# A score tile's maximum, minimum and squares one tile per step, with TensorE's side work between scores and weighted sum

## The chip, the cores and the metric

One core of one Trainium2 chip runs the kernel. The metric is the device time of one launch in microseconds (us).

## The reference

Sixteen sequences of 1024 token ids go through a small tower, in fp32:

```python
h = tok(x)          # embedding, 128x128, six gated convolutions (kernel 3), 128x128
h = h + attn(layernorm(h))
h = h + ffn(layernorm(h))

# attn: 8 heads of 16, two score maps
attn1 = softmax(q1 @ k1.T * scale); attn2 = softmax(q2 @ k2.T * scale)
# per window of 4 rows and head: mean, std, max, min over the 1024 keys of each map
gate_in = concat([window_stats(attn1, 4), window_stats(attn2, 4)])
alpha = sigmoid(mlp(gate_in))
out = ((alpha * attn1 + (1 - alpha) * attn2) @ v) @ Wo
```

The ffn part is a layer norm, a 128x128 product with a residual, one expert's two products with a gelu between, and a last product with a gelu.

## The kernel before

The five engines each run a program written out by hand; semaphores tie them together. The work on one sequence is a body of 128 steps: 16 units (8 heads, two score maps) of 8 row tiles of 128 queries. The loop runs over 16 sequences. Beside the attention of sequence i each step also carries side tasks: the tail of the sequence before (window statistics, gate, ffn: `POST`) and the front of the next one (embedding, convolutions `conva` and `convg`, q and k: `PRE`). `plan()` puts them into steps and isn't changed. It gives 95 of the 128 steps a side task on TensorE; steps 50 to 79 all have one.

A step n of the main work has these parts:
- `scores`: TensorE makes a 128x1024 score tile in one of two halves of `ps_s` (buffer n % 2), as two matmuls.
- `row_max`, `row_min` on VectorE: the tile's maximum and minimum. `squares` on ScalarE: exp of the tile minus its maximum, with its sum (`junk`, `sumsq`), an activation and a read of the accumulator.
- `scores_t`: TensorE makes the transposed scores of the tile 12 steps earlier in `ps_t`, again two matmuls; there is one `ps_t`. `exp_t` on ScalarE takes them to `exps`.
- `weighted`: TensorE multiplies `exps` of two steps earlier with v and adds into `ps_o`.
- side tasks of `STEP[n]`: on TensorE they write `ps_w`, a single bank. `wait_bank` makes each of them wait until the task before it has been read: by ScalarE (`va`, `ug`, `hpre`, `stage` and others) or, for eight kinds, by VectorE.

Before, two steps form a pair. VectorE takes both maxima, then both minima; ScalarE's squares stand between maximum and minimum of a tile. TensorE's order in a pair is scores, scores_t, scores, side task, scores_t, weighted twice, side task. A tile of `ps_s` is free for new scores when its minimum is through. `scores_t` and `exp_t` count in halves of 512 columns. SyncE's queue brings the units' q and k (12 transfers each) and the maxima as three rows (`mrow`); GpSimd has the elementwise part of the side tasks.

Of the kernel before, what the change touches and what calls it, by code (L numbers as in the profile page):

```python
# [24 lines left out]
P = 128  # L25
L = 1024
T = L // P
# [133 lines left out]
def tower_kernel(nc, ids, table, consts, w_e2h, b_e2h, conv_w, conv_b, w_h2e, b_h2e, wq1, wk1, wq2, wk2, wv, wo,  # L161
# [4 lines left out]
    with ExitStack() as ctx:  # L166
# [149 lines left out]
        def _(sp):  # L316
# [41 lines left out]
            with sp.Fori(0, NB // E) as group, sp.Fori(0, E) as e:  # L358
                i = group * E + e
                sp.wait_ge(s_emb, i * (16 * T) + 16 * T)  # L360
                settle()
                load_ids(i + 1)
                load_expert("body", i, e)
                for j in range(U):

                    if j:
                        sp.wait_ge(s_st, i * (2 * STEPS) + 2 * (T * (j - 3) + T - 1 + LAG_T) + 2)
                    else:
                        sp.wait_ge(s_exp, i * (2 * STEPS) + 2)
                    settle()  # L370
                    store_mrow("body", i, j)
                    if j + 1 in (U // 2, U):
                        wait_side(sp, "body", i, "pool", QK[(j + 1) % U // H][-1])
                        settle()
                    load_unit((j + 1) % U)
                    if ("gelu2",) in sum((STEP[n] for n in range(j * T, j * T + T)), []):
                        store_out("body", i)
# [7 lines left out]
        def _(pe):  # L385
# [3 lines left out]
            def scores(i, n):  # L389

                u, t = n // T, n % T
                if t == 0:
                    pe.wait_ge(s_ring[u % RING], i * (4 * 12 * 16) + 12 * 16 * (u // RING + 1))
                pe.wait_ge(s_min, i * STEPS + n + 1)
                for c in range(2):
# [4 lines left out]
            def scores_t(i, n):  # L400

                m = (n - LAG_T) % STEPS
                u, t = m // T, m % T
                if t == 0:
                    pe.wait_ge(s_mrow, i * (U * 64) + 64 * (n // T + 2))
                for c in range(2):
                    pe.wait_ge(s_exp, i * (2 * STEPS) + 2 * n + c + 1)
                    mm(ps_t[:, c, :], kst[:, u % RING, P * t:P * t + P], qst[:, u % RING, 512 * c:512 * c + 512])\
                        .then_inc(s_st, 1)

            def weighted(i, n, count=True):
# [3 lines left out]
                if count:  # L415
                    pe.wait_ge(s_exp, i * (2 * STEPS) + max(2 * n, 1))
                    if t == 0:
# [131 lines left out]
            with pe.Fori(0, NB // E) as group, pe.Fori(0, E) as e:  # L549
                i = group * E + e  # L550
                for n in range(0, STEPS, 2):
                    scores(i, n)
                    scores_t(i, n)
                    scores(i, n + 1)
                    for tk in STEP[n]:
                        task("body", i, tk)
                    scores_t(i, n + 1)
                    weighted(i, n)
                    weighted(i, n + 1)
                    for tk in STEP[n + 1]:  # L560
                        task("body", i, tk)
            for n in range(LAG_V):
# [8 lines left out]
        def _(act):  # L571
            def squares(i, n):

                r, t = n // T % RING, n % T
                if t == 0:

                    wait_side(act, "body", i, "pool", ("unit", n // T - 2) if n // T > 1 else None)
                act.wait_ge(s_max, i * STEPS + n + 1)
                act.wait_ge(s_sq, i * STEPS + n + 1)
# [3 lines left out]
            def exp_t(i, n):  # L583
                act.wait_ge(s_pv, i * STEPS + n + 1)
                for c in range(2):
                    act.wait_ge(s_st, i * (2 * STEPS) + 2 * n + c + 1)
                    nc.scalar.activation(exps[:, n % RING, 512 * c:512 * c + 512], ps_t[:, c, :], ACT.Exp,  # L587
                                         scale=0.5).then_inc(s_exp, 1)

# [89 lines left out]
            act.sem_inc(s_sq, 2)  # L679
            act.sem_inc(s_exp, 2)  # L680
            act.sem_inc(s_mrow, 64)
            for tk in PRE:
                task("pre", 0, tk)
            with act.Fori(0, NB // E) as group, act.Fori(0, E) as e:
                i = group * E + e
                for n in range(0, STEPS, 2):
                    exp_t(i, n)
                    squares(i, n)
                    for tk in STEP[n]:
                        task("body", i, tk)  # L690
                    squares(i, n + 1)
                    exp_t(i, n + 1)
                    for tk in STEP[n + 1]:
                        task("body", i, tk)
            for n in range(LAG_T):
# [6 lines left out]
        def _(dve):  # L702
# [17 lines left out]
            def row_min(i, n):  # L720
                r, t = n // T % RING, n % T
                dve.wait_ge(s_sq, i * STEPS + n + 3)
                nc.vector.tensor_reduce(rowmin[:, r, t:t + 1], ps_s[:, n % 2, :], axis=AX, op=ALU.min)\  # L723
# [106 lines left out]
            last.then_inc(s_init, 1)  # L830
            dve.sem_inc(s_min, 2)
            dve.sem_inc(s_out, 16)
# [5 lines left out]
            with dve.Fori(0, NB // E) as group, dve.Fori(0, E) as e:  # L838
                i = group * E + e
                for n in range(0, STEPS, 2):  # L840

                    row_max(i, n)
                    row_max(i, n + 1)
                    for tk in STEP[n]:
                        task("body", i, tk)
                    row_min(i, n)
                    row_min(i, n + 1)
                    for tk in STEP[n + 1]:
                        task("body", i, tk)
# [232 lines left out]
```

## Time and profile before

| | us |
|---|---|
| runs | 6308.97, 6310.05, 6312.23; median 6310.05 |
| span of the profiled execution | 6310.3 |
| TensorE, VectorE, ScalarE, GpSimd busy | 5419.2, 5358.7, 5292.3, 2425.1 |
| mean granted TensorE clock | 0.927 of full speed |

The profiled execution is one of its own; its span stands within 0.01% of the median of the runs, so sums against its times may be read against the runs as well. Times of the trace count from the start of the span. A granted clock of 1.00 is 2.4 GHz, 0.50 is 1.2 GHz.

### The profile page before, as it was taken

What the parts mean: (1) busy time and instruction counts of PE and PEld (TensorE: products, weight loads), DVE (VectorE), ACT (ScalarE), POOL (GpSimd) and SP (SyncE); (2) the same over time, 40 slices, a digit from 0 to 9 for tenths busy, and PEclk for the clock granted to TensorE, in tenths of its full rate; (3) what the DMA queues carried; (4) which work ended last, traced back from release to release, by engine and by line L of the source; (5) the groups of instructions that cost most, each with busy time, mean ns of one, the idle gap of its engine ahead of it and who ended that gap; (6) DMA issues with size and microseconds to landing.
All of it is one profiled execution on the core that took longest, in us unless ns stands there. A gap on an engine that the chain in (4) does not pass through costs nothing.

```text
span 6310.3 us, 127411 instructions
## 1 busy us (share of the span) xinstructions
PE 5419.2 (86%) x34070; PEld 2706.4 (43%) x34070; DVE 5358.7 (85%) x6524; ACT 5292.3 (84%) x9997; POOL 2425.1 (38%) x4629
## 2 busy tenths in 40 slices
PE   6988889889888888889889888888889888898886
PEld 4443434444343443434444343443434444343443
DVE  2888888898988888888898888888889888888883
ACT  2888888889888888888889888888888888888884
POOL 6424343342433424343342433424344242433422
PEclk8999989999998999989999898999999999898997
DMA  1001010010101001010010101001010010101000
GB/s 37 19 20 26 19 28 19 20 27 22 26 19 28 19 20 26 18 28 19 20 27 22 26 19 28 18 21 26 18 28 19 20 26 22 25 19 27 19 22 12
DMA packets 165102, 142.52 MB, mean 23 GB/s; under 512 B 89197, under 2 KB 108269, under 8 KB 164141
## 3 DMA queue, kind: packets, MB, share of 16 engines
q1 hardware_dynamic: 159100, 124.09, 8.5%
q0 software_dynamic: 4352, 8.92, 0.7%
q8 instruction: 325, 5.32, 0.4%
q14 instruction: 509, 4.16, 0.2%
q10 hardware_dynamic: 816, 0.02, 0.0%
HBM read 21.26 MB, written 8.91 MB: 5 GB/s over the span
## 4 chain that ended last, share of the span: by engine, by line
PE 40%; issue 22%; DVE 18%; ACT 14%; POOL 3%; ACTq 1%; SPq 1%; DMA 0%; DVEq 0%; POOLq 0%
PE ps_w L387 18%; PE ps_s L387 8%; DVE negmax L717 7%; PE ps_t L387 7%; ACT junk L580 7%; PE ps_o L387 6%; DVE rowmin L723 4%; ACT exps L587 4%; DVE o_t L732 1%; DVE bn L742 1%; ACT hpre L636 1%; DVE mean_all L736 1%; DVE recip L735 1%; PE ps_w L435 1%; SPq L329 1%
## 5 line engine op out<-in xcount | busy, mean ns | idle before, releaser
L723 DVE TENSOR_REDUCE rowmin<-ps_s 128x1 f32<-128x1024 f32 x2048 | 2479.1, 1221 | 559.8 <-ACT junk L580 468.0
L580 ACT ACTIVATE junk<-ps_s,negmax 128x1024 bf16<-128x1024 f32 x2048 | 2300.9, 1124 | 473.2 <-DVE negmax L717 438.2
L717 DVE TENSOR_REDUCE negmax<-ps_s 128x1 f32<-128x1024 f32 x2048 | 2412.9, 1215 | 156.0 <-PE ps_s L387 128.1
L587 ACT ACTIVATE exps<-ps_t 128x512 f32<-128x512 f32 x4120 | 2265.7, 615 | 230.7 <-PE ps_t L387 211.8
L387 PE MATMUL ps_s<-kst,qst 96*128 96x512 bf16 x4096 | 1329.3, 408 | 486.7 <-DVE rowmin L723 421.0
L387 PE MATMUL ps_t<-qst,kst 99*128 99x512 bf16 x4120 | 1442.9, 408 | 220.6 <-ACT exps L587 165.7
L387 PE MATMUL ps_w<-xc,cw 128*128 128x256 f32 x4704 | 1253.5, 404 | 22.0 <-ACT ug L656 12.4
L387 PE MATMUL ps_o<-exps,v_cur 128*32 128x256 f32 x16512 | 1161.6, 401 | 20.4 <-POOL v_cur L1012 20.3
L387 PEld LDWEIGHTS ps_w<-xc,cw 128*128 128x128 f32 x4704 | 902.8, 199 | 354.2 <-issue 117.2
L387 PEld LDWEIGHTS ps_t<-qst,kst 99*128 99x128 bf16 x4120 | 414.8, 101 | 1120.9 <-ACT exps L587 877.0
L871 POOL TENSOR_SCALAR ctmp<-ug 128x256 f32<-128x256 f32 x408 | 165.9, 407 | 1569.0 <-ACT ug L656 1561.0
L387 PEld LDWEIGHTS ps_s<-kst,qst 96*128 96x128 bf16 x4096 | 322.5, 101 | 1022.9 <-DVE rowmin L723 849.6
L387 PEld LDWEIGHTS ps_o<-exps,v_cur 128*32 128x32 f32 x16512 | 442.6, 112 | 634.1 <-issue 443.3
L580 ACT ACTIVATION_READ_ACCUMULATOR junk<-ps_s,negmax 128x1 f32 x2048 | 429.4, 210 | 0.0
L987 POOL TENSOR_TENSOR ctmp<-ctmp,va 128x256 f32<-128x256 f32 x408 | 296.7, 727 | 33.9
L988 POOL TENSOR_TENSOR ctmp<-ctmp,xc 128x256 f32<-128x256 f32 x408 | 278.8, 683 | 32.0
L884 POOL TENSOR_TENSOR dif_all<-rowmin,negmax 128x8 f32<-128x8 f32 x258 | 52.7, 204 | 578.9 <-DVE o_all L737 565.9
L591 ACT ACTIVATE va<-ps_w,cb 128x256 f32<-128x256 f32 x392 | 190.5, 486 | 61.8 <-PE ps_w L387 50.4
L656 ACT ACTIVATE ug<-ps_w,cb_half 128x256 f32<-128x256 f32 x392 | 190.7, 486 | 53.2 <-PE ps_w L387 51.3
L871 POOL TENSOR_SCALAR part<-stage 128x512 bf16<-128x512 f32 x132 | 82.1, 622 | 368.4 <-ACT stage L591 359.8
L871 POOL TENSOR_SCALAR xc<-ctmp 128x256 f32<-128x256 f32 x408 | 167.6, 411 | 65.3 <-POOL ctmp L988 65.3
L905 POOL DMA_INDIRECT att<-in_table,idx x136 | 131.5, 967 | 135.2 <-DMA idx<-in_ids 95.7
(179 smaller groups left out, 4147.6 us busy)
## 6 DMA issues: line engine op xcount, KB each, us to landing
qst<-part SPq DMA_DIRECT2D x1542, 32.0 KB, 2.0
kst<-part SPq DMA_DIRECT2D x1542, 32.0 KB, 2.0
qst<-mrow SPq DMA_DIRECT2D x1028, 1.5 KB
out_dram<-z SPq DMA_DIRECT2D x17, 512.0 KB, 3.2
fc1s<-in_fc_w SPq DMA_DIRECT2D x17, 256.0 KB
fc2s<-in_fc_w SPq DMA_DIRECT2D x17, 256.0 KB
cw<-in_conv_w SPq DMA_DIRECT2D x1, 2304.0 KB
att<-in_table,idx POOLq DMA_INDIRECT x136
```

Source lines behind the costliest of these rows:

```text
L329: sp.dma_start(dst[HD * g:HD * g + HD, r, :], part[HD * h:HD * h + HD, a, w, c, :])\
L387: return nc.tensor.matmul(dst, lhs, rhs, start=start, stop=stop, **kw)
L580: nc.scalar.activation(junk[:, n % 2, :], ps_s[:, n % 2, :], ACT.Exp, bias=negmax[:, r, t:t + 1], accum_out=sumsq[:, r, t:t + 1]).then_inc ...
L587: nc.scalar.activation(exps[:, n % RING, 512 * c:512 * c + 512], ps_t[:, c, :], ACT.Exp, scale=0.5).then_inc(s_exp, 1)
L591: return nc.scalar.activation(dst, src, ACT.Identity, **kw)
L656: last = nc.scalar.activation(ug[:, c % 2, :], bank[:, CH:2 * CH], ACT.Tanh, scale=0.5, bias=cb_half[:, 2 * l + 1:2 * l + 2])
L717: nc.vector.tensor_reduce(negmax[:, r, t:t + 1], ps_s[:, n % 2, :], axis=AX, op=ALU.max, negate=True)\
L723: nc.vector.tensor_reduce(rowmin[:, r, t:t + 1], ps_s[:, n % 2, :], axis=AX, op=ALU.min)\
L871: return nc.gpsimd.tensor_scalar(*args)
L905: nc.gpsimd.indirect_dma_start(out=emb[:, t, :], out_offset=None, in_=table[:, :], in_offset=bass.IndirectOffsetOnAxis(ap=idx[:, t:t + 1], ...
L987: chain(i, tt(ctmp[:, 1, :], ctmp[:, 0, :], va[:, c % 2, :], ALU.mult))
L988: chain(i, tt(ctmp[:, 2, :], ctmp[:, 1, :], x_in, ALU.add))
```

## The change

A tile now goes maximum, minimum, squares, and a step is one tile. VectorE's `row_min` no longer waits for anything of its own (it follows `row_max` on the same tile); `squares` waits for the minimum; `scores` waits for the squares of two steps earlier, which now is the last reader of the tile. `scores_t` and `exp_t` are counted once for a step; `exp_t` is one activation of 1024 columns instead of two of 512. TensorE's order in each step is scores, side tasks, weighted, scores_t; ScalarE's is exp_t, side tasks, squares. The initial counts and SyncE's waits follow.

```diff
--- before.py
+++ after.py
@@ -364,9 +364,9 @@
                 for j in range(U):
 
                     if j:
-                        sp.wait_ge(s_st, i * (2 * STEPS) + 2 * (T * (j - 3) + T - 1 + LAG_T) + 2)
+                        sp.wait_ge(s_st, i * STEPS + T * (j - 3) + T + LAG_T)
                     else:
-                        sp.wait_ge(s_exp, i * (2 * STEPS) + 2)
+                        sp.wait_ge(s_exp, i * STEPS + 1)
                     settle()
                     store_mrow("body", i, j)
                     if j + 1 in (U // 2, U):
@@ -391,7 +391,7 @@
                 u, t = n // T, n % T
                 if t == 0:
                     pe.wait_ge(s_ring[u % RING], i * (4 * 12 * 16) + 12 * 16 * (u // RING + 1))
-                pe.wait_ge(s_min, i * STEPS + n + 1)
+                pe.wait_ge(s_sq, i * STEPS + n + 1)
                 for c in range(2):
                     last = mm(ps_s[:, n % 2, 512 * c:512 * c + 512], qst[0:KSC, u % RING, P * t:P * t + P],
                               kst[0:KSC, u % RING, 512 * c:512 * c + 512])
@@ -403,17 +403,18 @@
                 u, t = m // T, m % T
                 if t == 0:
                     pe.wait_ge(s_mrow, i * (U * 64) + 64 * (n // T + 2))
+                pe.wait_ge(s_exp, i * STEPS + n + 1)
                 for c in range(2):
-                    pe.wait_ge(s_exp, i * (2 * STEPS) + 2 * n + c + 1)
-                    mm(ps_t[:, c, :], kst[:, u % RING, P * t:P * t + P], qst[:, u % RING, 512 * c:512 * c + 512])\
-                        .then_inc(s_st, 1)
+                    last = mm(ps_t[:, c, :], kst[:, u % RING, P * t:P * t + P],
+                              qst[:, u % RING, 512 * c:512 * c + 512])
+                last.then_inc(s_st, 1)
 
             def weighted(i, n, count=True):
 
                 m = (n - LAG_V) % STEPS
                 h, t = m // T % H, m % T
                 if count:
-                    pe.wait_ge(s_exp, i * (2 * STEPS) + max(2 * n, 1))
+                    pe.wait_ge(s_exp, i * STEPS + max(n, 1))
                     if t == 0:
                         pe.wait_ge(s_ot, i * U + n // T + 1)
                     if m == 0:
@@ -548,17 +549,12 @@
             wait_side(pe, "body", 0, "dve")
             with pe.Fori(0, NB // E) as group, pe.Fori(0, E) as e:
                 i = group * E + e
-                for n in range(0, STEPS, 2):
+                for n in range(STEPS):
                     scores(i, n)
-                    scores_t(i, n)
-                    scores(i, n + 1)
                     for tk in STEP[n]:
                         task("body", i, tk)
-                    scores_t(i, n + 1)
                     weighted(i, n)
-                    weighted(i, n + 1)
-                    for tk in STEP[n + 1]:
-                        task("body", i, tk)
+                    scores_t(i, n)
             for n in range(LAG_V):
                 if n < LAG_T:
                     scores_t(NB, n)
@@ -575,17 +571,16 @@
                 if t == 0:
 
                     wait_side(act, "body", i, "pool", ("unit", n // T - 2) if n // T > 1 else None)
-                act.wait_ge(s_max, i * STEPS + n + 1)
+                act.wait_ge(s_min, i * STEPS + n + 1)
                 act.wait_ge(s_sq, i * STEPS + n + 1)
                 nc.scalar.activation(junk[:, n % 2, :], ps_s[:, n % 2, :], ACT.Exp, bias=negmax[:, r, t:t + 1],
                                      accum_out=sumsq[:, r, t:t + 1]).then_inc(s_sq, 1)
 
             def exp_t(i, n):
                 act.wait_ge(s_pv, i * STEPS + n + 1)
-                for c in range(2):
-                    act.wait_ge(s_st, i * (2 * STEPS) + 2 * n + c + 1)
-                    nc.scalar.activation(exps[:, n % RING, 512 * c:512 * c + 512], ps_t[:, c, :], ACT.Exp,
-                                         scale=0.5).then_inc(s_exp, 1)
+                act.wait_ge(s_st, i * STEPS + n + 1)
+                nc.scalar.activation(exps[:, n % RING, :], ps_t[:, :, :].rearrange("p c q -> p (c q)"), ACT.Exp,
+                                     scale=0.5).then_inc(s_exp, 1)
 
             def ident_act(dst, src, **kw):
                 return nc.scalar.activation(dst, src, ACT.Identity, **kw)
@@ -677,21 +672,17 @@
             nc.scalar.activation(cb_half[:, :], cb[:, :], ACT.Copy, scale=0.5).then_inc(s_init, 1)
             act.wait_ge(s_init, 4)
             act.sem_inc(s_sq, 2)
-            act.sem_inc(s_exp, 2)
+            act.sem_inc(s_exp, 1)
             act.sem_inc(s_mrow, 64)
             for tk in PRE:
                 task("pre", 0, tk)
             with act.Fori(0, NB // E) as group, act.Fori(0, E) as e:
                 i = group * E + e
-                for n in range(0, STEPS, 2):
+                for n in range(STEPS):
                     exp_t(i, n)
-                    squares(i, n)
                     for tk in STEP[n]:
                         task("body", i, tk)
-                    squares(i, n + 1)
-                    exp_t(i, n + 1)
-                    for tk in STEP[n + 1]:
-                        task("body", i, tk)
+                    squares(i, n)
             for n in range(LAG_T):
                 exp_t(NB, n)
             for tk in TAIL:
@@ -719,7 +710,6 @@
 
             def row_min(i, n):
                 r, t = n // T % RING, n % T
-                dve.wait_ge(s_sq, i * STEPS + n + 3)
                 nc.vector.tensor_reduce(rowmin[:, r, t:t + 1], ps_s[:, n % 2, :], axis=AX, op=ALU.min)\
                     .then_inc(s_min, 1)
 
@@ -828,7 +818,6 @@
 
             last = nc.vector.memset(kst[KSC:KST, :, :], 1.0)
             last.then_inc(s_init, 1)
-            dve.sem_inc(s_min, 2)
             dve.sem_inc(s_out, 16)
             dve.wait_ge(s_load, 16 * N_LOADS)
             dve.wait_ge(s_init, 4)
@@ -837,15 +826,10 @@
             pos.update(loop=True, base=pos["n"], n=0, per=U + 3)
             with dve.Fori(0, NB // E) as group, dve.Fori(0, E) as e:
                 i = group * E + e
-                for n in range(0, STEPS, 2):
-
+                for n in range(STEPS):
                     row_max(i, n)
-                    row_max(i, n + 1)
+                    row_min(i, n)
                     for tk in STEP[n]:
-                        task("body", i, tk)
-                    row_min(i, n)
-                    row_min(i, n + 1)
-                    for tk in STEP[n + 1]:
                         task("body", i, tk)
             assert pos["n"] == pos["per"], pos
             pos.update(n=0)
```

What the order on TensorE looks like, before, where a convolution half (`ps_w<-xc,cw`) and a product of fc1 (`ps_w<-xa,fc1s`) stand in neighbouring steps, about the middle of the body (REGISTER_ALU and ISA rows work out and make waits):

```order
L394 REGISTER_ALU
L387 MATMUL ps_s<-kst,qst 128x512 x2
L273 REGISTER_ALU
L387 MATMUL ps_w<-xc,cw 128x256 x3
L407 REGISTER_ALU
L387 MATMUL ps_t<-qst,kst 128x512
L407 REGISTER_ALU
L387 MATMUL ps_t<-qst,kst 128x512
L387 MATMUL ps_o<-exps,v_cur 32x256 x8
L273 REGISTER_ALU
L387 MATMUL ps_w<-xa,fc1s 128x256 x2
```

And after the change, at such a place:

```order
L387 MATMUL ps_s<-kst,qst 128x512 x2
L273 REGISTER_ALU x2
L387 MATMUL ps_w<-xc,cw 128x256 x3
L419 REGISTER_ALU
L387 MATMUL ps_o<-exps,v_cur 32x256 x4
L387 MATMUL ps_t<-qst,kst 128x512 x2
L394 REGISTER_ALU
L387 MATMUL ps_s<-kst,qst 128x512 x2
L273 REGISTER_ALU
L387 MATMUL ps_w<-xa,fc1s 128x256 x2
L387 MATMUL ps_o<-exps,v_cur 32x256 x4
L387 MATMUL ps_t<-qst,kst 128x512 x2
```

The matmuls of weighted (`ps_o`) and of scores_t (`ps_t`) stood between the two side tasks for both steps of the pair; now scores_t of step n and scores of step n + 1 stand ahead of the side task of step n + 1, and weighted and scores_t of that step behind it.

ScalarE, before, the same two tasks' activations (`ug` for the convolution half, `hpre` for fc1):

```order
L580 ACTIVATE junk,sumsq<-ps_s,negmax 128x1024
L273 REGISTER_ALU
L656 ACTIVATE ug<-ps_w,cb_half 128x256
L578 REGISTER_ALU
L580 ACTIVATE junk,sumsq<-ps_s,negmax 128x1024
L586 REGISTER_ALU
L587 ACTIVATE exps<-ps_t 128x512
L586 REGISTER_ALU
L587 ACTIVATE exps<-ps_t 128x512
L273 REGISTER_ALU
L591 ACTIVATE hpre<-ps_w,fc1bs 128x256 x2
```

And after (line numbers are those of the changed file):

```order
L582 ACTIVATE exps<-ps_t 128x1024
L273 REGISTER_ALU
L651 ACTIVATE ug<-ps_w,cb_half 128x256
L576 ACTIVATE junk,sumsq<-ps_s,negmax 128x1024
L580 REGISTER_ALU
L582 ACTIVATE exps<-ps_t 128x1024
L273 REGISTER_ALU
L586 ACTIVATE hpre<-ps_w,fc1bs 128x256 x2
L576 ACTIVATE junk,sumsq<-ps_s,negmax 128x1024
```

The activation that reads the side bank stood behind the squares in the first step of a pair and behind exp_t in the second; now it stands behind exp_t in every step.

## Rows read from the trace of the kernel before

**Rows 1.** The page: span, engines, granted clock by slice

```profile
span 6310.3 us, 127411 instructions
...
PE 5419.2 (86%) x34070; PEld 2706.4 (43%) x34070; DVE 5358.7 (85%) x6524; ACT 5292.3 (84%) x9997; POOL 2425.1 (38%) x4629
...
PEclk8999989999998999989999898999999999898997
```

**Rows 2.** Busy time in four stretches; each row begins with the stretch and its length

```profile
core 0: us, PE busy (x) PEld busy (x) DVE busy (x) ACT busy (x) POOL busy (x), PEclk, DMA share, GB/s
0.00:138.30 138.30, 82.60 (x367) 65.86 (x368) 17.00 (x43) 29.48 (x61) 86.35 (x135) 0.86 0.12 31
3168.80:3548.00 379.20, 329.77 (x2092) 162.35 (x2090) 332.86 (x402) 327.91 (x619) 144.54 (x279) 0.94 0.10 23
3312.30:3396.30 84.00, 81.35 (x522) 44.88 (x520) 74.77 (x79) 77.75 (x157) 27.18 (x62) 0.98 0.09 20
6202.70:6310.30 107.60, 56.32 (x330) 37.31 (x330) 12.89 (x51) 37.15 (x66) 25.94 (x31) 0.71 0.03 10
```

**Rows 3.** The list of waits: who waited for whom, µs, times, longest

```profile
PEld ps_s L387 <- DVE rowmin L723: 849.6, 1306, 4.3
...
ACT junk L580 <- DVE negmax L717: 438.2, 484, 2.6
...
PEld ps_w L387 <- ACT va L591: 70.3, 104, 0.9
```

**Rows 4.** Timeline with side work in every step: start, length, engine, line

```profile
3384.56 1.01 ACT L591 ACTIVATE hpre<-ps_w,fc1bs 128x256 f32<-128x256 f32 x2
...
3385.04 2.35 DVE L717 TENSOR_REDUCE negmax<-ps_s 128x1 f32<-128x1024 f32 x2
...
3385.22 0.60 PE L387 MATMUL ps_s<-kst,qst 96*128 96x512 bf16 x2
...
3385.28 1.26 ACT L587 ACTIVATE exps<-ps_t 128x512 f32<-128x512 f32 x2
3385.63 1.16 PEld L387 LDWEIGHTS ps_w<-xc,cw 128*128 128x128 f32 x6 [0.30 <-ACT hpre L591]
3385.66 1.53 PE L387 MATMUL ps_w<-xc,cw 128*128 128x256 f32 x6
...
3386.29 1.26 ACT L580 ACTIVATE junk<-ps_s,negmax 128x1024 bf16<-128x1024 f32 x1
...
3387.03 0.60 PE L387 MATMUL ps_t<-qst,kst 99*128 99x512 bf16 x2
...
3387.31 0.34 ACT L580 ACTIVATION_READ_ACCUMULATOR junk<-ps_s,negmax 128x1 f32 x1
3387.40 0.61 ACT L656 ACTIVATE ug<-ps_w,cb_half 128x256 f32<-128x256 f32 x1
...
3387.55 1.07 PE L387 MATMUL ps_o<-exps,v_cur 128*32 128x256 f32 x16
...
3388.55 1.13 PE L387 MATMUL ps_w<-xa,fc1s 128*128 128x256 f32 x4
...
3388.84 1.24 ACT L587 ACTIVATE exps<-ps_t 128x512 f32<-128x512 f32 x2
...
3389.52 0.60 PE L387 MATMUL ps_s<-kst,qst 96*128 96x512 bf16 x2
...
3389.80 1.01 ACT L591 ACTIVATE hpre<-ps_w,fc1bs 128x256 f32<-128x256 f32 x2
```

**Rows 5.** The costliest groups on the page: busy µs, mean ns

```profile
L656 ACT ACTIVATE ug<-ps_w,cb_half 128x256 f32<-128x256 f32 x392 | 190.7, 486 | 53.2 <-PE ps_w L387 51.3
```

**Rows 6.** Timeline at gelu1 and just behind it

```profile
3398.99 1.28 ACT L636 ACT_TABLE_LOAD   x1
...
3400.29 3.89 ACT L636 ACTIVATE hpre<-hpre 128x1024 f32<-128x1024 f32 x4
...
3408.98 2.77 PE L387 MATMUL ps_w<-xc,cw 128*128 128x256 f32 x6
```

## The prediction

> **What bounds the kernel now.** I read the page's shares first: VectorE, ScalarE and TensorE are busy 85, 84 and 86% of a span of 6310.3 us, so no engine is the bound by itself; what counts is how they wait for each other [rows 1]. The stretches come next: a prologue of 138.3 us, a tail of 107.6 us, and between them 16 equal blocks of 379.2 us, 128 steps each, 2.96 us a step [rows 2]. One stretch inside a block is of special use: steps 50 to 79, in each of which TensorE has a side task, take 84.0 us, 2.80 us a step [rows 2].
>
> The list of waits says where the order bites: scores wait for the row minimum (849.6 us), the squares for the row maximum (438.2 us) [rows 3]. The timeline shows one pair of steps: both maxima (2.35 us), squares, squares, minimum, minimum. The reader is to see in it that TensorE hardly ever waits for its side bank ps_w. The convolution at 3385.66 started 0.09 us after the end of the hpre activation that empties the bank (3384.56 + 1.01), and the weight load had waited 0.30 us for it [rows 4]. Over the whole run such a wait for the va activations costs 70.3 us in 104 times [rows 3]: it is nearly free, because the pairwise order leaves a whole step between the read of the bank and the next task.
>
> **The change part by part.**
>
> *Score order.* VectorE now runs maximum and minimum of one tile, 2.35 us for two such reductions [rows 4], and the squares come last. A tile's circle is scores, maximum, minimum, squares: 0.64 + 2.35 + 0.04 + 1.36 + 0.05 us. 0.64 is 0.60 for two matmuls [rows 4] and a hand-over of 0.04; 1.36 is from the squares' start to the end of the accumulator's read (3386.29 to 3387.65) [rows 4]. That is 4.4 us over two tiles, so the score engine pair could run at 2.35 us a step. The waits of [rows 3] on rowmin go away as such.
>
> *Merged exponential.* Two activations of 512 columns become one of 1024. The two take 0.96 us until the next activation starts (3388.84 to 3389.80) [rows 4]; four activations of 128x1024 take 3.89 us with a last one of about a full length, so at most 0.97 us each [rows 6]. I cost the merge at nothing. The bounds: the merged one may need 0.96 or, by the squares' length, 1.26 us [rows 4]; the far end is 0.3 us a step dearer. A step on the Trainium skill, apart from the sum: ScalarE: Activation LUTs, section "What ACT_TABLE_LOAD costs", puts an activation with immediate operands at 186 ns plus 0.833 ns an element, with 93 ns of overlap. By that an estimate of two halves is 1.04 us and of one whole 0.95 us, which would give back about 0.09 us a step; the trace's 0.96 against at most 0.97 doesn't bear this out.
>
> *One instead of two counts for the halves.* scores_t now waits for the whole of the previous exponential and the exponential for both matmuls of scores_t. Before, the halves were handed over one by one. From the start of scores_t to that of the exponential it is now 0.64 us (0.60 for two matmuls and 0.04) [rows 4].
>
> *TensorE's side work.* This decides, and it is the step where I expect the loss. The new order on TensorE is scores, side task, weighted, scores_t; on ScalarE exponential, side task, squares. There is one side bank ps_w, and each task on TensorE waits until the previous task's reader is through. So where steps n and n+1 both have a task that ScalarE reads, there is a circle of ONE step: scores_t(n), exponential(n), ScalarE's side task(n), then TensorE's side task(n+1), weighted(n+1), scores_t(n+1). Queued behind the waiting side task are weighted and scores_t, and the next exponential waits for those. Its price, all from [rows 4] unless said:
> - 0.64 scores_t to exponential; 0.96 exponential to the side activation;
> - the side activation: 0.49 (ug) [rows 5], or 1.01 for the two of hpre;
> - 0.06 hand-over (0.09 at most, above);
> - TensorE's task: 1.37 for a convolution half (3385.66 to 3387.03), 0.97 for fc1 (3388.55 to 3389.52);
> - 0.50 weighted, half of the 1.00 from 3387.55 to 3388.55.
>
> Convolution behind convolution: 0.64 + 0.96 + 0.49 + 0.06 + 1.37 + 0.50 = 4.02 us. fc1 behind convolution 3.62, convolution behind fc1 4.54, mean 4.08. Of the 127 neighbouring steps in the plan, 69 are such a pair with ScalarE as the first one's reader: 20 convolution behind convolution, 15 mixed with fc1, 34 others, whose TensorE tasks are mostly transposes or single products; for those I take the 3.62 us of the cheaper form. The mean is (35 x 4.05 + 34 x 3.62) / 69 = 3.84 us, against 2.80 us a step now [rows 2]. That is 69 x 1.04 = 72 us a block.
>
> *The other 59 steps.* They cost 379.2 - 69 x 2.80 = 186 us now. After the change 38 of them alternate, one with a task and one without: the circle over two steps is squares' end, scores 0.44 (3385.22 to 3385.66), task 1.37, weighted 0.50, then 0.64 + 0.96 + 0.49 and squares 1.36, with 0.05 of hand-over 5.8 us, a bit less with the smaller tasks; call it 2.75 us a step, 105. Seven follow a task that VectorE reads (2.75, 19). Fourteen have nothing beside them and go at VectorE's 2.35 (33). To these 157 us come the long activations with their table loads (3.89 + two of 1.28 for gelu1) [rows 6], the moments on VectorE and the slow clock behind such pauses. What they cost now is what is left of the 186 us when 59 steps have 2.62 us each (5.24 for two, 3384.56 to 3389.80) [rows 4]: about 31 us, and I keep 30. Sum 187 us: no change. Prologue and tail keep their work.
>
> *Pool, queues.* The DMAs are the same. SP's waits for scores_t and the exponential name the same steps in new counts. GpSimd's msplit has three reductions instead of four between its maximum and VectorE's mrow, over 3.5 us (three of 2.35 / 2) [rows 4], and the loads go out a whole unit of 8 steps ahead; with longer steps they have more time, not less. I cost them at nothing.
>
> *Sum.* 16 x 72 = 1150 us on top of the profiled execution's 6310.3 us gives 7460 us; the median of the runs is 6310.05, so the same number stands against it.
>
> **TensorE's clock.** Behind the gelu1 pause a convolution's six matmuls took 2.77 us [rows 6] instead of 1.53 us [rows 4]. In the new circle TensorE has 0.44 + 0.44 + 1.37 + 0.50 us to issue in 4.02 us, so it idles about 1.2 us in each. If the clock falls to 1.2 GHz there, scores_t, task and weighted roughly double and a step costs about 6.3 us. TensorE: Matmul & The Clock Gate, section "HAM oscillation — how this bites in real kernels", warns of regular idle gaps on TensorE, which is D below as a rule; no row here has this pattern. Now TensorE idles 13% of a block (329.77 of 379.20 us busy) and the granted clock is 0.94; where side work is dense it idles 3% at 0.98 [rows 2]. Neither shows what 30% in short pieces does, so D below gets a small chance and no more.
>
> **The rivals.**
> - *A, forecast:* the one-step circle through ps_w. 0.81.
> - *B, the bank wait doesn't bind* and only the two-step circle over the squares does (5.8 us for two steps, 2.9 against 2.80 now): 16 x 69 x 0.1 = +110, 6420 us, perhaps 6300 with what light steps give. For it: the wait is just 70.3 us now [rows 3]. Against: ScalarE's task moved behind the exponential that TensorE's own later work feeds. 0.06.
> - *C, faster:* ps_w is free in time and VectorE alone sets the pace: its own work in the 30 dense steps is 74.8 of 84.0 us, 0.31 us a step less [rows 2]; 16 x 69 x 0.31 = -340, so 5970 us. It decides if the side task on TensorE could start before about 2.3 us of the step are gone; here it would have to be free 1.5 us earlier than the sum says. 0.05.
> - *D, the clock falls in the runs:* a third of 69 steps at 6.3 instead of 3.84 us gives 16 x 57 = 900 on top, 8370 us. 0.08.
>
> **How the numbers follow.** Predicted 7460 us. The circle's bounds: 3.62 us if all links are of the cheap form (+900, 7210), 4.4 us if the merged exponential takes 0.3 us more and hpre's 1.01 is frequent (+1770, 8080); a gain of 0.1 us in the 59 other steps is -95. I take 7100 to 7850, which leaves B, C and D outside. A measurement of this kernel tells about 0.2% from no change. Faster has C and a sliver of B: 0.06; same 0.02; slower 0.92.
>
> **What would show it.** Right: a step of about 4 us in the stretch where side work is dense (30 steps in about 117 instead of 84.0 us); matmuls or weight loads of ps_w that wait for ScalarE's va, ug, hpre for over a microsecond each, the largest sum in the list of waits; VectorE's wait for ScalarE before rowmin gone; VectorE's share down from 85 to about 72% (85 x 6310 / 7460); steps without side work at 2.4 us. Wrong: ps_w loads that start as soon as scores are issued; or a granted clock far under 0.93, which would be D.

## The result and the profile after

The changed kernel takes 7757.4 us (median of 4 runs, 7751.06 to 7773.02), the kernel before beside it on the same chip 6309.51: a ratio of 1.2297, with a 95% interval of 1.228 to 1.2315. The forecast was 7460 us, 7100 to 7850. The profiled execution has a span of 7760.3 us at a mean granted clock of 0.940 (0.927 before).

The page of the changed kernel, to be held against [rows 1]; the L rows give busy us, mean ns, and the idle time ahead with who ended it:

```profile
span 7760.3 us, 118934 instructions
...
PE 5667.7 (73%) x34070; PEld 2477.9 (32%) x34070; DVE 5320.7 (69%) x6524; ACT 5171.0 (67%) x7937; POOL 2419.8 (31%) x4629
...
PEclk8999999999999999999999999999999999999898
...
L582 ACT ACTIVATE exps<-ps_t 128x1024 f32<-128x1024 f32 x2060 | 2112.8, 1026 | 2261.4 <-PE ps_t L387 2258.2
L713 DVE TENSOR_REDUCE rowmin<-ps_s 128x1 f32<-128x1024 f32 x2048 | 2488.4, 1215 | 0.0
```

VectorE and ScalarE have the same work as before, within 2.5%, over a longer span. What the change meant for VectorE it got: rowmin waits for nothing. But the exponentials now wait 2261 us in all, for scores_t.

The stretches of the changed kernel, one block and steps 50 to 79 of it, to be held against [rows 2]:

```profile
3880.70:4349.50 468.80, 345.92 (x2090) 148.63 (x2092) 330.67 (x403) 319.00 (x489) 144.41 (x279) 0.94 0.08 18
4059.90:4183.60 123.70, 86.95 (x509) 40.59 (x512) 74.80 (x81) 76.80 (x126) 27.05 (x62) 0.97 0.06 14
```

A block went from 379.2 to 468.8 us, and 16 x 89.6 = 1434 of the 1450 us between the two profiled executions. The 30 steps with dense side work alone went from 84.0 to 123.7 us. VectorE and ScalarE have the same 75 and 77 us of work there as before.

The list of waits, changed kernel, to be held against [rows 3]:

```profile
POOL ctmp L855 <- ACT ug L651: 2525.0, 369, 15.9
ACT exps L582 <- PE ps_t L387: 2258.2, 1518, 19.9
DVE negmax L708 <- PE ps_s L387: 2085.5, 1325, 19.8
PEld ps_s L387 <- ACT junk L576: 868.4, 643, 6.1
...
PEld ps_w L387 <- ACT va L586: 473.7, 304, 1.6
...
PE ps_w L387 <- ACT ug L651: 363.9, 336, 1.3
...
PEld ps_w L387 <- ACT ug L651: 319.9, 208, 1.7
PE ps_w L387 <- ACT va L586: 318.5, 304, 1.1
```

The wait of a ps_w weight load for va rose from 70.3 to 473.7 us. The first row is GpSimd, 31% busy, waiting for its next piece of side work. The next two look like TensorE being slow. They aren't: TensorE is idle 27% of the span. These rows pass on what TensorE itself waited for. All rows in which a matmul on ps_w waits for a ScalarE activation add up to 1260 us, against 98 before; for the weight loads of ps_w it is 1362 us against 224. Only a timeline shows where such a wait begins. Here is one pair of steps of the changed kernel, to be held against [rows 4], the idle time ahead in brackets:

```profile
4122.25 0.60 PE L387 MATMUL ps_t<-qst,kst 99*128 99x512 bf16 x2
...
4122.69 0.60 PE L387 MATMUL ps_s<-kst,qst 96*128 96x512 bf16 x2
...
4122.95 1.02 ACT L582 ACTIVATE exps<-ps_t 128x1024 f32<-128x1024 f32 x1 [1.45 <-PE ps_t L387]
...
4123.88 0.84 ACT L586 ACTIVATE hpre<-ps_w,fc1bs 128x256 f32<-128x256 f32 x2
...
4124.76 1.56 PE L387 MATMUL ps_w<-xc,cw 128*128 128x256 f32 x6 [1.47 <-ACT hpre L586]
...
4126.26 0.64 PE L387 MATMUL ps_o<-exps,v_cur 128*32 128x256 f32 x8
...
4126.83 0.61 PE L387 MATMUL ps_t<-qst,kst 99*128 99x512 bf16 x2
...
4127.53 1.02 ACT L582 ACTIVATE exps<-ps_t 128x1024 f32<-128x1024 f32 x1 [1.72 <-PE ps_t L387]
...
4128.45 0.47 ACT L586 ACTIVATE va<-ps_w,cb 128x256 f32<-128x256 f32 x1
...
4128.97 1.13 PE L387 MATMUL ps_w<-xa,fc1s 128*128 128x256 f32 x4 [1.11 <-ACT va L586]
...
4130.03 0.64 PE L387 MATMUL ps_o<-exps,v_cur 128*32 128x256 f32 x8
...
4130.61 0.61 PE L387 MATMUL ps_t<-qst,kst 99*128 99x512 bf16 x2
```

Read it as a ring (the prediction's circle through ps_w): scores_t, exponential, the activation that empties the bank, the next task on the bank, weighted, scores_t. No link has slack. TensorE stands 1.47 us ahead of one task and 1.11 ahead of the other. One round took 4.58 us (4122.25 to 4126.83), the next 3.78.

### The profile page after: what moved, and what is told of

Its sections match the earlier page's. It is cut to its first block, busy times and chain, and to the rows that moved or that the text cites. A ratio compares the mean times of both kernels' runs of the same rounds, so it can differ in the third digit from the quotient of the medians.

```text
span 7760.3 us, 118934 instructions
## 1 busy us (share of the span) xinstructions
PE 5667.7 (73%) x34070; PEld 2477.9 (32%) x34070; DVE 5320.7 (69%) x6524; ACT 5171.0 (67%) x7937; POOL 2419.8 (31%) x4629
## 3 DMA queue, kind: packets, MB, share of 16 engines
q14 instruction: 462, 3.78, 0.2%
## 4 chain that ended last, share of the span: by engine, by line
PE 51%; issue 21%; ACT 15%; DVE 6%; POOL 3%; ACTq 2%; SPq 1%; DMA 1%; POOLq 0%; DVEq 0%
PE ps_w L387 23%; PE ps_o L387 12%; PE ps_t L387 11%; PE ps_s L387 4%; DVE rowmin L713 3%; ACT ug L651 2%; ACT junk L576 2%; ACT exps L582 2%; ACT va L586 2%; ACT hpre L586 1%; SPq L329 1%; PE ps_w L436 1%; DVE negmax L708 1%; ACT stage L586 1%; DVE bn L732 1%
## 5 line engine op out<-in xcount | busy, mean ns | idle before, releaser
L708 DVE TENSOR_REDUCE negmax<-ps_s 128x1 f32<-128x1024 f32 x2048 | 2502.1, 1222 | 2093.3 <-PE ps_s L387 2085.5
L582 ACT ACTIVATE exps<-ps_t 128x1024 f32<-128x1024 f32 x2060 | 2112.8, 1026 | 2261.4 <-PE ps_t L387 2258.2
L387 PE MATMUL ps_w<-xc,cw 128*128 128x256 f32 x4704 | 1310.0, 418 | 627.7 <-ACT va L586 186.1
L387 PE MATMUL ps_o<-exps,v_cur 128*32 128x256 f32 x16512 | 1401.1, 413 | 80.8 <-DVE o_t L722 60.5
L387 PE MATMUL ps_t<-qst,kst 99*128 99x512 bf16 x4120 | 1301.5, 399 | 69.5 <-ACT exps L582 67.5
L387 PEld LDWEIGHTS ps_o<-exps,v_cur 128*32 128x32 f32 x16512 | 334.3, 111 | 868.8 <-issue 674.3
L387 PEld LDWEIGHTS ps_t<-qst,kst 99*128 99x128 bf16 x4120 | 237.2, 98 | 1010.9 <-issue 747.9
L855 POOL TENSOR_SCALAR mparts<-negmax 128x8 bf16<-128x8 f32 x256 | 51.8, 202 | 664.2 <-DVE negmax L708 631.5
L387 PE MATMUL ps_w<-xa,fc1s 128*128 128x256 f32 x524 | 147.3, 404 | 144.6 <-ACT ug L651 73.9
L722 DVE STREAM_TRANSPOSE o_t<-ps_o 128x256 f32<-128x256 f32 x258 | 115.0, 446 | 112.9 <-PE ps_o L387 110.8
L586 ACT ACTIVATE va<-ps_w,cb 128x256 f32<-128x256 f32 x392 | 184.5, 471 | 10.8 <-POOL xc L855 8.3
```

The costliest lines, as they stand in the source:

```text
L387: return nc.tensor.matmul(dst, lhs, rhs, start=start, stop=stop, **kw)
L582: nc.scalar.activation(exps[:, n % RING, :], ps_t[:, :, :].rearrange("p c q -> p (c q)"), ACT.Exp, scale=0.5).then_inc(s_exp, 1)
L586: return nc.scalar.activation(dst, src, ACT.Identity, **kw)
L708: nc.vector.tensor_reduce(negmax[:, r, t:t + 1], ps_s[:, n % 2, :], axis=AX, op=ALU.max, negate=True)\
L722: nc.vector.transpose(o_t[:, :], ps_o[:, 0:QC]).then_inc(s_ot, 1)
L855: return nc.gpsimd.tensor_scalar(*args)
```

## The experiments

Each ratio is against the kernel before on the same chip; the median of the kernel before was about 6380 us in the runs of x1 to x4 and x12, and 6306 to 6309 in the others. Edits are against the changed kernel unless said. a2 is the changed kernel again, on the chip of x9 and x10; x5 to x8 ran on another chip, whose kernel before stands within 0.1% of a2's.

**a2_changed_again.** 

> The changed kernel as it is, on the same chip as the other two of this set, so that small differences can be read: ratio 1.23 of the kernel before.

Measured: 7768.83 us, ratio 1.2312 (1.2291 to 1.2332). The result repeats.

**x1_side_behind_scores_t**, the ring opened on TensorE:

```diff
                     scores(i, n)
-                    for tk in STEP[n]:
-                        task("body", i, tk)
                     weighted(i, n)
                     scores_t(i, n)
+                    for tk in STEP[n]:
+                        task("body", i, tk)
```

> The changed kernel with one edit: TensorE's side task stands behind scores_t instead of between scores and weighted. If the one-step circle through ps_w is the cause (forecast A), it opens, because ScalarE has the whole of the next step's exponential, scores and weighted to empty the bank: a step with side work falls from 4.2 us to TensorE's own 2.8 us (0.44 + 0.5 + 0.44 + 1.4), a block from 468 to about 375 us, the whole to 6150 to 6400 us. If the two-step circle over the squares is the cause (B), little changes, since squares still stand behind the side task: 7400 to 7800 us.

Measured: 6220.53 us, ratio 0.9738 (0.9709 to 0.9766). Steps 50 to 79, and a step of them:

```profile
3268.70:3348.60 79.90, 76.75 (x508) 41.23 (x512) 74.18 (x81) 77.06 (x127) 26.98 (x61) 1.00 0.10 21
```

```profile
3300.89 0.61 PE L387 MATMUL ps_t<-qst,kst 99*128 99x512 bf16 x2
...
3301.34 1.46 PE L387 MATMUL ps_w<-xc,cw 128*128 128x256 f32 x6
...
3301.60 1.02 ACT L582 ACTIVATE exps<-ps_t 128x1024 f32<-128x1024 f32 x1 [0.47 <-PE ps_t L387]
...
3302.91 0.48 ACT L586 ACTIVATE va<-ps_w,cb 128x256 f32<-128x256 f32 x1 [0.29 <-PE ps_w L387]
```

The time lies in the 6150 to 6400 us expected of an open ring. The task now runs beside the exponential instead of behind it. The 30 steps went from 123.7 to 79.9 us, with the same instructions. Over the whole run the matmuls on ps_w wait 10 us for ScalarE, not 1260.

**x2_act_side_first**, the ring opened on ScalarE instead:

```diff
-                    exp_t(i, n)
                     for tk in STEP[n]:
                         task("body", i, tk)
+                    exp_t(i, n)
                     squares(i, n)
```

> The changed kernel with one edit on the other engine: ScalarE does its side task ahead of exp_t, TensorE's order stays. If the circle through ps_w is the cause, the link scores_t to exponential to side activation leaves it, the bank is read right behind TensorE's task, and the time falls to 6200 to 6600 us, near x1. If instead TensorE's side task costs because it delays scores_t itself, the time stays above 7000 us.

Measured: 6315.99 us, ratio 0.9887 (0.9858 to 0.9916). The side activation goes ahead of the exponential, and the loss is gone too. Two edits on two engines, with no line in common, each take back all of it; what they share is the ring. TensorE's side task still stands ahead of scores_t in x2, so its place there alone isn't what costs.

**x5_dose_in_circle and x6_dose_outside.** One more activation of 128x256, in the 48 steps with a convolution: in x5 ahead of the side activation, inside the ring, in x6 behind it, ahead of the squares. (The line that declares the buffer `extra` is left out here.)

```diff
                     exp_t(i, n)
+                    if any(tk[0] in ("conva", "convg") for tk in STEP[n]):      # x5
+                        nc.scalar.activation(extra[:, n % 4, :], cw[:, 0, 0, :], ACT.Copy)
                     for tk in STEP[n]:
                         task("body", i, tk)
+                    # x6: the two lines here instead
                     squares(i, n)
```

> The changed kernel with one activation more (128x256, of a weight into an unused buffer) on ScalarE in each of the 48 steps with a convolution half, between exp_t and the side activation, so inside the circle through ps_w. 42 of these steps are followed by a step with a task on TensorE. By the circle each costs 0.36 us more: 16 x 42 x 0.36 = 242 us, ratio 1.265 to 1.27 of the kernel before. If ScalarE's order is not in the circle, ratio 1.23.

> The same activation in the same steps, but behind the side activation and ahead of squares: ScalarE does exactly the same work as in the other dose kernel, outside the one-step circle through ps_w. If that circle is the cause, ratio 1.23 to 1.24. If the two-step circle over the squares is the bound, it costs as much as inside.

Measured: x5 8150.93 us, ratio 1.2932 (1.291 to 1.2953); x6 7780.39 us, ratio 1.2351 (1.2317 to 1.2385). On one chip, x5 takes 371 us more than x6 for the same work. Against a2, x6 pays 12 us, which is within the spread of its own runs (7760.70 to 7807.64), and x5 382 us. In the timeline of x5:

```profile
4266.98 1.02 ACT L583 ACTIVATE exps<-ps_t 128x1024 f32<-128x1024 f32 x1 [1.79 <-PE ps_t L388]
...
4267.90 0.41 ACT L685 ACTIVATE extra<-cw 128x256 bf16<-128x256 f32 x1
4268.21 0.47 ACT L587 ACTIVATE va<-ps_w,cb 128x256 f32<-128x256 f32 x1
```

The dose moves va by 0.31 us (1.23 us behind the exponential's start instead of 0.92 above). As the expectation says, 42 of the 48 steps are followed by a step with a task on TensorE; by the starts of scores_t, these 42 transitions are 0.30 us longer than in the changed kernel (the median of the 42). 16 x 42 x 0.30 is 202 us, the ring's part. But x5's ratio stands above the expected 1.265 to 1.27, and its profiled execution is 349 us longer than the changed kernel's (8109.0 against 7760.3), so some 147 us are something else. A good part is TensorE's clock. Two stretches of x5 hold the same work, three transitions that begin with that from step 30 to 31, in one block and in the next:

```profile
3671.40:3682.20 10.80, 7.91 (x54) 3.88 (x50) 6.67 (x8) 7.68 (x13) 4.02 (x9) 1.00 0.01 2
4153.40:4169.80 16.40, 14.35 (x55) 6.29 (x52) 7.29 (x8) 7.69 (x13) 6.87 (x10) 0.51 0.02 5
```

At a granted clock of 0.51 they took 5.6 us longer than at 1.00; in the changed kernel they took 10.2 or 10.6 us in every block. Against 10.8 us this place alone costs x5 70 us over the 16 blocks. An estimate for the whole, from the mean clocks 0.921 and 0.940: (1 - clock) x 2 x span is the time at the low level, 1281 against 931 us. Work done in those 350 us takes twice as long at most, so up to 175 us more. Why the clock fell more in x5 isn't shown.

**x10_scores_twice.** The two score matmuls are issued twice in the 76 steps where this step and the one before have a task on TensorE, 0.44 us more work ahead of the waiting task.

```diff
-                for c in range(2):
+                on_pe = lambda m: any(tk[0] in COST for tk in STEP[m])
+                for c in (0, 1, 0, 1) if n and on_pe(n - 1) and on_pe(n) else (0, 1):
```

> The changed kernel with the two score matmuls issued twice, into the same place, in the 76 steps where this and the step before have a task on TensorE. That fills 0.44 us of the 1.2 us in which TensorE waits for the bank and adds nothing to the circle through ps_w. If idle pieces lower the clock and so make a part of the loss, the granted clock rises above 0.94 and the ratio falls to 1.21 to 1.225. If the waits alone are the cause, ratio 1.23; if scores are on the circle after all, up to 16 x 76 x 0.44 = 535 us more, ratio 1.31.

Measured: 7734.84 us, ratio 1.2259 (1.2239 to 1.228), clock 0.951. TensorE's extra work disappears in its wait: TensorE isn't the bound, and scores aren't in the ring. The ratio lies between the two expectations, 1.23 and 1.21 to 1.225: against a2 the higher clock goes with 0.4%, and the two intervals just miss each other.

**x4_halves_restored.** scores_t and exp_t count in halves again.

```diff
-                pe.wait_ge(s_exp, i * STEPS + n + 1)
                 for c in range(2):
-                    last = mm(ps_t[:, c, :], kst[:, u % RING, P * t:P * t + P],
-                              qst[:, u % RING, 512 * c:512 * c + 512])
-                last.then_inc(s_st, 1)
+                    pe.wait_ge(s_exp, i * (2 * STEPS) + 2 * n + c + 1)
+                    mm(ps_t[:, c, :], kst[:, u % RING, P * t:P * t + P], qst[:, u % RING, 512 * c:512 * c + 512])\
+                        .then_inc(s_st, 1)
...
-                act.wait_ge(s_st, i * STEPS + n + 1)
-                nc.scalar.activation(exps[:, n % RING, :], ps_t[:, :, :].rearrange("p c q -> p (c q)"), ACT.Exp,
-                                     scale=0.5).then_inc(s_exp, 1)
+                for c in range(2):
+                    act.wait_ge(s_st, i * (2 * STEPS) + 2 * n + c + 1)
+                    nc.scalar.activation(exps[:, n % RING, 512 * c:512 * c + 512], ps_t[:, c, :], ACT.Exp,
+                                         scale=0.5).then_inc(s_exp, 1)
```

The counts elsewhere follow.

> The changed kernel with the exponential and scores_t counted and done in halves of 512 columns again. By the circle, the exponential starts 0.2 us earlier behind scores_t and ends at the latest 0.1 us later for the two instructions: a gain of 0.1 to 0.25 us in each of 69 x 16 circles, so 7480 to 7650 us. If the merge was free or a gain, 7750 us or more.

Measured: 7546.36 us, ratio 1.1813 (1.1778 to 1.1848); a block 456.8 us. In its timeline:

```profile
4012.31 0.60 PE L387 MATMUL ps_t<-qst,kst 99*128 99x512 bf16 x2
...
4012.74 1.09 ACT L582 ACTIVATE exps<-ps_t 128x512 f32<-128x512 f32 x2 [1.03 <-PE ps_t L387]
...
4013.71 0.48 ACT L586 ACTIVATE xa<-ps_w,col 128x256 f32<-128x256 f32 x1
```

The exponential starts 0.43 us behind scores_t, not 0.70 (4122.25 to 4122.95 above), since it needs the first half alone; to the side activation it is then 0.97 instead of 0.93. That is 0.23 us a round, and 16 x 69 x 0.23 = 254 us. The starts of scores_t say the same: the 69 transitions of a block took 284 us, not 299. Measured are 211 us by the raw medians and 305 by the ratios; the two kernels ran on chips that differ by 1%. So the merge cost 2.7 to 3.9% of this kernel's time.

**x3_score_order_alone**, an edit of the kernel before: the pairs, the halves and all places of side work stay; only a tile's maximum, minimum, squares change their order.

```diff
-                pe.wait_ge(s_min, i * STEPS + n + 1)
+                pe.wait_ge(s_sq, i * STEPS + n + 1)
...
-                act.wait_ge(s_max, i * STEPS + n + 1)
+                act.wait_ge(s_min, i * STEPS + n + 1)
...
-                dve.wait_ge(s_sq, i * STEPS + n + 3)
...
-            dve.sem_inc(s_min, 2)
...
                     row_max(i, n)
-                    row_max(i, n + 1)
+                    row_min(i, n)
                     for tk in STEP[n]:
                         task("body", i, tk)
-                    row_min(i, n)
+                    row_max(i, n + 1)
                     row_min(i, n + 1)
```

> The kernel before with the other part of the change alone: maximum, minimum, then squares, still in pairs of steps with the side work and the exponentials where they were before. If the new order of the score tile itself is harmless or good, 6000 to 6400 us; if it carries a good part of the loss, above 6700 us. I expect some loss from squares of both tiles now coming late for the next pair's scores: 6450 us.

Measured: 7184.17 us, ratio 1.1252 (1.1218 to 1.1285), clock 0.889. The guess was 6450 us; this is the case in which the new order carries a good part of a loss, when it is put into the old pairs. In its timeline:

```profile
3836.14 1.22 DVE L722 TENSOR_REDUCE rowmin<-ps_s 128x1 f32<-128x1024 f32 x1
...
3837.39 1.11 ACT L580 ACTIVATE junk<-ps_s,negmax 128x1024 bf16<-128x1024 f32 x1 [0.55 <-DVE rowmin L722]
...
3838.49 1.07 ACT L587 ACTIVATE exps<-ps_t 128x512 f32<-128x512 f32 x2
...
3839.14 0.88 PE L387 MATMUL ps_t<-qst,kst 99*128 99x512 bf16 x2 [0.18 <-ACT exps L587]
...
3839.85 0.60 PE L387 MATMUL ps_s<-kst,qst 96*128 96x512 bf16 x2
```

The second squares of a pair wait for the second minimum; the second exponential is queued behind them, the next scores_t waits for it, and the next pair's second scores are queued behind that. This is a ring too, through ps_t.

**x12_order_alone_exp_first**, x3 with the second exp_t of a pair ahead of the second squares.

```diff
-                    squares(i, n + 1)
                     exp_t(i, n + 1)
+                    squares(i, n + 1)
```

> x3 (the new score order alone, in pairs) with one edit: ScalarE does the second exponential of a pair ahead of its second squares. In x3's trace those squares wait for the second minimum, the exponential stands behind them, the next scores_t waits for it, and the second scores are queued behind that scores_t. If that circle makes the 12.5% of x3, the time falls back to 0.98 to 1.03 of the kernel before. If it stays above 1.08, the new order of the score tile costs by itself.

Measured: 6655.78 us, ratio 1.0434 (1.0414 to 1.0454), clock 0.923. Two thirds of x3's loss was the ring through ps_t. The remaining 4.3% fit neither expectation and stay open. What x12's list of waits shows is that weight loads for scores now wait 1020.8 us for the squares, where before they waited 849.6 us for the minimum.

**x7_behind_scores_t_halves and x8_act_first_halves**: the edit of x1 or of x2, each with that of x4.

> TensorE's side task behind scores_t as in x1, and the exponentials in halves again. With the circle through ps_w gone, the halves' earlier start is worth something only where scores_t to exponential bounds: ratio 0.95 to 0.975 of the kernel before, against 0.974 for the side task alone.

> ScalarE's side task ahead of exp_t as in x2, and the halves again. TensorE still makes scores_t last in its step, so exponential and next squares wait for it: I expect more from the halves here than behind scores_t, ratio 0.955 to 0.985, against 0.989.

Measured: x7 6112.89 us, ratio 0.9691 (0.9675 to 0.9707), a block of 367.2 us, the best of all; x8 6188.3 us, 0.9806 (0.9789 to 0.9823). Both lie in the expected ranges. By the ratios the halves are worth 0.5% behind x1 and 0.8% behind x2, where the ring is open, against 3.9% where it is closed (x4). By the raw medians, across chips that differ by 1%, it is 1.7 and 2.0% against 2.7%. Either way they are worth more in the closed ring.

**x9_halves_squares_first**: x7, and ScalarE's order is exp_t, squares, side tasks.

```diff
                     exp_t(i, n)
+                    squares(i, n)
                     for tk in STEP[n]:
                         task("body", i, tk)
-                    squares(i, n)
```

> The fastest version so far (side task behind scores_t on TensorE, halves) with ScalarE's side tasks moved behind squares. The squares no longer wait for a long side task such as gelu1, so scores go on beside it; where nothing is long, the bank is emptied later but TensorE comes back to it only behind the next scores_t: ratio 0.955 to 0.97 of the kernel before, against 0.969. If the later read of the bank binds again, above 0.98.

Measured: 6659.13 us, ratio 1.0561 (1.0543 to 1.0579), a block of 399.5 us. The bank binds again, the case of the expectation above 0.98. Matmuls on ps_w wait 362 us for ScalarE, against 10 in x7:

```profile
3419.53 1.11 ACT L575 ACTIVATE junk<-ps_s,negmax 128x1024 bf16<-128x1024 f32 x1 [0.63 <-DVE rowmin L713]
...
3420.64 0.47 ACT L586 ACTIVATE va<-ps_w,cb 128x256 f32<-128x256 f32 x1
...
3421.15 1.08 PE L387 MATMUL ps_w<-hid,g 128*64 128x256 f32 x4 [0.33 <-ACT va L586]
```

The squares wait for the minimum, the bank's reader stands behind them, and the task waits for the reader.

## Why the prediction was right, by its steps

The circle through ps_w is the cause. It is seen in the timeline; opened from either side it gives back all of the loss (x1, x2); the same dose costs 382 us inside it and 12 us, within the noise, beside it (x5, x6); and work that isn't in it is free (x10). That x1, x2 and x6 came out as they did leaves no room for rival B, the circle over the squares. What each step said and what was measured:

| step | forecast | measured |
|---|---|---|
| scores_t to exponential | 0.64 | 0.70 |
| exponential to side activation | 0.96 | 0.92, 0.93 |
| side activation, ug or va / hpre | 0.49 / 1.01 | 0.47 / 0.84 |
| hand-over to TensorE | 0.06 | 0.04, 0.05 |
| TensorE's task, convolution / fc1 | 1.37 / 0.97 | 1.50 / 1.06 |
| weighted | 0.50 | 0.57, 0.58 |
| convolution behind fc1 / fc1 behind convolution | 4.54 / 3.62 | 4.58 / 3.78 |
| steps 50 to 79 | 117 | 123.7 |
| a step without side work | 2.35 | 2.57 in the middle; 2.27 where VectorE sets the pace |
| VectorE's share | 72% | 69% |

- **One-step circle, 3.84 us a transition: right in kind, too small.** The starts of scores_t in the trace give the 69 transitions of a block 299 us, 4.3 us each, some 15 us of it pauses such as gelu1's; without those about 4.1. It is the term that was mis-sized: 69 x (4.1 - 3.84) = 18 us, just the block's 89.6 instead of 72 us. The smaller part is in the links: TensorE's task and weighted were taken from rows in which the next work followed at once, and with a wait ahead each took 0.07 to 0.13 us more. Convolution behind convolution took 4.21 us in the middle, not 4.02. The larger part is in the 34 other transitions, priced at the cheapest form, 3.62 us, as transposes or single products. By the plan 21 of them have a convolution on one side, 7 as the task that TensorE waits to start. Their medians by kind are 3.79, 3.90 and 4.28 us (convolution first, none, convolution second), 3.93 on average; 34 x 0.31 is 11 of the 18 us.
- **The merge costed at nothing: wrong.** The bounds weighed one long activation against two short ones. Its duration was indeed no dearer (1026 ns mean, 0.93 us until the next starts). What it costs is the early hand-over of the first half, 0.2 us of every round (x4). The forecast of 0.64 us had that wait in it, but it was never set against the 0.4 us that halves would have needed, so the sum held the cost without saying so.
- **The other 59 steps, no change: right.** 468.8 less 69 x 4.1 and the 15 us of pauses leaves about 171 us; with the pauses 186, as before. The 38 alternating ones, forecast at 105 us, took 105.
- **The list of waits, ps_w for ScalarE as the largest sum: wrong.** The rows are split by reader and by load or matmul; even added up, the 1362 us of loads or 1260 of matmuls stay under exps and negmax, onto which they are passed, with over 2000 us each. Waits of over a microsecond for va, ug and hpre are there.
- **Rivals B and C.** B is out by 1300 us. C was wrong of this kernel. With the ring open the kernel is faster than before, as C would have it, but not at VectorE's pace: x7 stands at 6113 us, not 5970, and in x1's dense stretch TensorE is busy 76.75 of 79.90 us, VectorE 74.18.
- **Rival D, the clock falls: no.** Time at the low level, worked out as for x5, is 931 us after and 921 before. TensorE idled 27% of the span, most of it in pieces of over a microsecond, at a mean clock of 0.940. TensorE: Matmul & The Clock Gate of the Trainium skill, "HAM oscillation — how this bites in real kernels", tells of a kernel whose clock fell again in each regular gap; its gaps, waits for DMA, are longer than the 1.1 to 1.5 us here, so this run doesn't speak against it. Where the low level falls into the ring it hurts as foreseen. Six matmuls of a convolution that took 1.56 us at 4124.76 took 2.51 here, at a granted clock of 0.60:

```profile
4062.54 2.51 PE L387 MATMUL ps_w<-xc,cw 128*128 128x256 f32 x6 [0.67 <-ACT ug L651]
```

x5, with longer gaps, did lose clock, and that was D on a small scale.

In short: all of the loss came with where the side work went, and the merge made it larger. The order maximum, minimum, squares with one tile a step is no hindrance: with it, side work behind scores_t and halves, x7 is 3.1% faster than the kernel before. How much of that is the order's own isn't shown; put alone into the old pairs it was slower (x3, x12).

## What to carry to other kernels

Before moving work on an in-order engine, draw the ring through each single buffer: who writes it, who empties it, and what is queued between the two on both engines; its length bounds the step, whatever the shares of busy time say. Put the writer right behind the work that another engine then needs (x1), so that this work isn't queued behind the wait for the buffer. And a merge of two instructions is only free if nobody waits for the first half.

## What the hardware showed that was not expected

- TensorE idle 27% of the time, mostly in short pieces, kept a mean granted clock of 0.940. With the same work packed to 96% busy in x1's dense stretch (76.75 of 79.90 us against 86.95 of 123.70) it was 1.00 against 0.97. x5's gaps, 0.3 us longer, went with 0.921, and with 0.51 in the stretch shown above.
- One activation of 1024 columns took 1.02 us, two of 512 took 1.08 to 1.09 from the first start to the last end: a merge saves 0.06 us of ScalarE's time, less than the early hand-over gives.
- VectorE's two reductions of a tile took 2.27 us a step where nothing else bound them, 0.08 us less than their busy time read from [rows 4]: the next maximum starts before the minimum's time is out.

```profile
4281.33 1.23 DVE L708 TENSOR_REDUCE negmax<-ps_s 128x1 f32<-128x1024 f32 x1 [0.25 <-PE ps_s L387]
4282.47 1.22 DVE L713 TENSOR_REDUCE rowmin<-ps_s 128x1 f32<-128x1024 f32 x1
4283.60 1.22 DVE L708 TENSOR_REDUCE negmax<-ps_s 128x1 f32<-128x1024 f32 x1
```

Not tried: a second side bank beside ps_w.
